# A state-space layer with a tree layer behind it on one core: constant products, the first delta, two broadcasts and the last leaf stages take other places

## What is computed

```python
h = layernorm(x) * (1 + ca) + sa
xp, z = split(h @ W_in)                       # 256 channels each
u = silu(causal_depthwise_conv(xp))           # 4 taps
dt_r, Bm, Cm = split(u @ W_xp, [8, 24])       # 8, 16 and 16 columns
delta = softplus(dt_r @ W_dt + dt_bias)
# for each channel e and each of 16 states n, over the 2048 positions t:
#   state = exp(-delta * exp(A_log)) * state + delta * Bm * u;   y = sum_n state * Cm
x = x + ga * ((y + u * D_skip) * silu(z)) @ W_out
h = layernorm(x) * (1 + cb) + sb
gate = sigmoid(h @ Wq.T @ routers.T)          # 255 nodes of a binary tree of depth 8
leaf_prob = product of gate or 1 - gate along the path to each of 256 leaves
x = x + gb * (leaf_prob @ leaf_values @ Wout_w.T + Wout_b)
```

## Time and profile before

| | |
|---|---|
| median of 3 runs (lowest, highest) | 488.26 us (485.96, 488.31) |
| the profiled execution, its span | 488.33 us, 486.5 us |
| VectorE busy | 447.5 us, 92% of the span |
| GpSimd busy | 422.0 us, 87% |
| TensorE busy with products | 404.0 us, 83% |
| ScalarE busy | 377.1 us, 77% |
| mean granted TensorE clock | 0.961 of full speed |

### The profile page before, as it was taken

How to read it: one execution, slowest core, us unless ns; L and a number is a source line. 1 busy time by engine, 2 the same in 40 slices (tenths; PEclk the granted TensorE clock), 3 DMA queues, 4 the chain that set the end, 5 groups by cost and what they waited for, 6 DMA issues and landing times. The chain is left out here.

```text
span 486.5 us, 6739 instructions
## 1 busy us (share of the span) xinstructions
PE 404.0 (83%) x2164; PEld 274.6 (56%) x2164; DVE 447.5 (92%) x539; ACT 377.1 (77%) x690; POOL 422.0 (87%) x236
## 2 busy tenths in 40 slices
PE   6979765997679887997889888997789887688596
PEld 3546544584547545584647546574647555566374
DVE  6687999999999999999999899989999899999872
ACT  4376985499777998698967999699966997777825
POOL 6148899999999989999899889999899889999910
PEclk9979997899799999999989999999999998799999
DMA  6684019200632019300633018300632027300001
GB/s 168 159 279 182 1 30 343 88 0 1 232 140 88 1 22 350 113 0 2 217 154 109 2 34 340 108 2 0 247 143 93 1 54 319 108 2 22 0 1 43
DMA packets 24146, 51.06 MB, mean 105 GB/s; under 512 B 4521, under 2 KB 14256, under 8 KB 20016
## 3 DMA queue, kind: packets, MB, share of 16 engines
q1 hardware_dynamic: 24112, 50.64, 30.4%
HBM read 48.01 MB, written 2.62 MB: 104 GB/s over the span
## 5 line engine op out<-in xcount | busy, mean ns | idle before, releaser
L606 POOL TENSOR_TENSOR hc<-h,c_rows 128x1024 f32<-128x1024 f32 x127 | 297.9, 2364 | 23.8 <-DVE h L1382 22.7
L1382 DVE TENSOR_TENSOR_SCAN h<-dA,state,dbu 128x512 f32<-128x512 f32 x192 | 234.0, 1270 | 7.3 <-ACT dA L697 7.3
L697 ACT ACTIVATE dA<-delta,a_neg 128x512 f32<-128x512 f32 x256 | 172.7, 684 | 38.1 <-DVE h L1382 37.7
L1123 PEld LDWEIGHTS yb<-ident,hc 128*128 128x128 f32 x1024 | 127.8, 146 | 65.5 <-issue 40.8
L1123 PE MATMUL yb<-ident,hc 128*128 128x128 f32 x1024 | 151.4, 282 | 12.6 <-POOL hc L606 12.6
L1395 DVE TENSOR_TENSOR dbu<-du,bb 128x1024 f32<-128x1024 f32 x88 | 105.9, 1203 | 6.6 <-PE bb L1148 5.8
L593 POOL TENSOR_TENSOR dbu<-du,b_rows 128x1024 f32<-128x1024 f32 x40 | 94.6, 2365 | 4.4 <-DMA b_rows<-bc_dram 4.4
L1382 DVE TENSOR_TENSOR_SCAN h<-dA,dbu 128x512 f32<-128x512 f32 x64 | 74.2, 1209 | 2.7 <-ACT dA L697 2.6
L1148 PE MATMUL bb<-b_parts,sel 128*128 128x512 bf16 x88 | 35.0, 398 | 34.5 <-DVE dbu L1395 33.2
L1023 PE MATMUL mf<-f_hT,w_conv 128*128 128x512 f32 x112 | 55.0, 616 | 1.8 <-ACT zu L757 1.2
L1148 PEld LDWEIGHTS bb<-b_parts,sel 128*128 128x128 bf16 x88 | 8.8, 100 | 47.3 <-DVE dbu L1395 27.8
(11 more groups left out here) (207 smaller groups left out, 520.5 us busy)
## 6 DMA issues: line engine op xcount, KB each, us to landing
...
```

What stands on the lines that cost most here:

```text
L606: nc.gpsimd.tensor_tensor(hc[:, pair % RC, :, :], h[:, pair % RH, :, :], c_rows[:, q, n % NQ, :].unsqueeze(1).broadcast_to([P, HALVES, T]) ...
L697: nc.scalar.activation(dA[ke % RD][:, :], delta[:, ge % 2, half, :], ACT.Exp, scale=a_neg[:, half, n:n + 1]).then_inc(s_dA, 1)
L1123: last = nc.tensor.matmul(bank[:, tile], hc[:, pair % RC, half, tile], ident[:, :], start=False, stop=n == N - 1, is_transpose=True, skip_ ...
L1382: v.tensor_tensor_scan(h[:, pair % RH, half, :], dA[k % RD][:, :], dbu[:, pair % RW, half, :], start, ALU.mult, ALU.add).then_inc(s_scan, 1)
```

## The change

It has four parts. (1) The preparation of group 0: eleven instead of seven start products, and further ones of the same kind ("fillers") behind the modulation products, the turn of x, ahead of the first fill and, in group 7's tail, where the leaf product's second half was. The second group of modulation products, the gate products and the folding move from between and behind the u products to behind the xd product, the folding to behind the first fill; the folded matrix is copied by ScalarE ahead of its third exponential. The first two deltas come from the eight dt rows of xd and W_dt as it is (`w_dt8`; rows 32 to 39), for which two DMAs are added. ScalarE copies xd before VectorE casts it, and VectorE casts from that copy. (2) The gate values are worked out at step 19 of group 0 (`S_GATES`). (3) The fills of pairs 3 and 4 are issued at k = 1 and 4 instead of 3 and 5 (`SOONER`). (4) In group 7 the leaf stages of group 5 go to the f side, at steps 4 to 9 instead of 12 to 16; group 6's tail comes two steps sooner, and its leaf product is all issued within the loop. Waits and reads that name the side (`leaf_side`, `due`) follow.

The diff, with repeated renamings of the side left out:

```diff
@@ -68,7 +68,7 @@
...
-    B_HI, C_ROW, B_MID, B_LO = 0, N, 64, 96
+    B_HI, C_ROW, DT_ROW, B_MID, B_LO = 0, N, 32, 64, 96
@@ -103,20 +103,23 @@
...
-    WARM_START = 7
+    WARM_START = 11
+    S_GATES = 19
+    SOONER = {1: 3, 4: 4}
...
     BY_HAND = 1
-    LAST_T = (("yt", 0, -1, (6,)), ("yt", 1, -1, (8,)), ("out", 0, -1, (10,)), ("lp", 0, -2, (12,)),
-              ("lp", 1, -2, (14,)), ("ff", 0, -2, (16,)), ("tr", 0, -1, (19,)), ("node", 0, -1, (21,)),
-              ("node", 1, -1, (23,)), ("lp", 0, -1, (27,)), ("lp", 1, -1, (29,)), ("ff", 0, -1, (STEPS,)))
-    LAST_SP = {2: -2, 25: -1}
+    LAST_T = (("yt", 0, -1, (6,)), ("yt", 1, -1, (8,)), ("out", 0, -1, (10,)), ("tr", 0, -1, (17,)),
+              ("node", 0, -1, (19,)), ("node", 1, -1, (21,)), ("lp", 0, -1, (25,)), ("lp", 1, -1, (27,)),
+              ("ff", 0, -1, (29, 30)))
+    LAST_F = (("lp", 0, -2, (4,)), ("lp", 1, -2, (6,)), ("ff", 0, -2, (8, 9)))
+    LAST_SP = {2: -2, 23: -1}
     TOKENS = (slice(0, T // 2), slice(T // 2, T))
-    LAST_STATS, LAST_RSTD, LAST_OFF, LAST_XHAT = 14, 16, 16, 17
+    LAST_STATS, LAST_RSTD, LAST_OFF, LAST_XHAT = 13, 14, 14, 15
...
-        if side == "t" and g == LAST:
-            return LAST_T
+        if g == LAST:
+            return LAST_T if side == "t" else LAST_F
@@ -158,6 +166,7 @@
...
         w_dt = sb("w_dt", [R, DI])
+        w_dt8 = sb("w_dt8", [DT_ROW + R, DI])
@@ -390,7 +399,7 @@
...
-        n_late, n_dt, n_col, n_xp, n_rest = 2, 2, 4, 4, 14
+        n_late, n_dt, n_col, n_xp, n_rest = 2, 2, 4, 6, 14
@@ -424,8 +433,9 @@
...
             sp.wait_ge(s_wz, 1)
-            for row, first, width in ((B_HI, R, N), (C_ROW, R + N, N), (B_MID, R, N), (B_LO, R, N)):
+            for row, first, width in ((DT_ROW, 0, R), (B_HI, R, N), (C_ROW, R + N, N), (B_MID, R, N), (B_LO, R, N)):
                 load(w_xp[:, :, row:row + width], xp_v[:, :, first:first + width], s_wxp)
+            load(w_dt8[DT_ROW:DT_ROW + R, :], W_dt, s_wxp)
@@ -668,7 +678,7 @@
...
                 nc.scalar.preload_act_table_set("softplus")
-                act.wait_ge(s_hi, 1)
+                act.wait_ge(s_xd0, 1)
@@ -693,6 +703,12 @@
...
                             act.wait_ge(s_aneg, 1)
+                            act.wait_ge(s_gatec, 1)
+                        if ke == 2:
+                            act.wait_ge(s_wdtp, 1)
+                            nc.scalar.activation(w_xdt[:, :, :],
+                                                 dA[2][:, 0:HALVES * DI].rearrange("p (h e) -> p h e", h=HALVES),
+                                                 ACT.Copy).then_inc(s_wdt, 1)
@@ -852,10 +870,6 @@
...
                 nc.scalar.preload_act_table_set("softplus")
-                wait_job(act, "t", "ff", 0, t - 1)
-                nc.scalar.activation(xs[:, (t - 1) * TILES:t * TILES, :],
-                                     job("t", "ff", 0, t - 1)[1][:, :].rearrange("p (i d) -> p i d", d=DM),
-                                     ACT.Copy).then_inc(s_read["t"], 1)
@@ -910,7 +924,7 @@
...
                 for hh in range(HALVES):
-                    last = nc.tensor.matmul(dA[0][:, hh * DI:(hh + 1) * DI], w_dtin_t[:, hh * P:(hh + 1) * P],
+                    last = nc.tensor.matmul(dA[2][:, hh * DI:(hh + 1) * DI], w_dtin_t[:, hh * P:(hh + 1) * P],
@@ -927,25 +941,21 @@
...
             def dt_product(half):
-                for hh in range(HALVES):
-                    last = nc.tensor.matmul(yb[half][:, :], w_xdt[:, hh, half * P:(half + 1) * P],
-                                            zu[:, 0, HALVES + hh, :], start=hh == 0, stop=hh == HALVES - 1)
-                last.then_inc(s_dt0, 1)
+                nc.tensor.matmul(yb[half][:, :], w_dt8[DT_ROW:DT_ROW + R, half * P:(half + 1) * P],
+                                 xd[DT_ROW:DT_ROW + R, :], start=True, stop=True).then_inc(s_dt0, 1)
...
                 modulation_products(yb[0], 0)
+                keep_warm_on(dA[0], 1)
...
                 turn_x(mb["f"][0], s_tr0)
-                dt_weight_transposes()
+                keep_warm_on(dA[0], 2)
...
                 u_product(0)
-                pe.wait_ge(s_wlate, 16 * n_late)
-                modulation_products(mb["t"][0], 3)
-                dt_weight_products()
+                dt_weight_transposes()
                 u_product(1)
-                gate_products()
@@ -953,13 +963,16 @@
...
                 last.then_inc(s_xd0, 1)
-                pe.wait_ge(s_wdt, 1)
-                dt_product(0)
+                pe.wait_ge(s_wlate, 16 * n_late)
+                modulation_products(mb["t"][0], 3)
+                gate_products()
...
                 pe.wait_ge(s_xdc, 1)
+                pe.wait_ge(s_modc, 1)
+                dt_product(0)
+                pe.wait_ge(s_hi, 1)
...
                                  skip_group_check=True).then_inc(s_r1, 1)
-                pe.wait_ge(s_gatec, 1)
@@ -1043,6 +1056,8 @@
...
                         pe.wait_ge(s_silu, g + 1)
+                        if (side, g) == ("f", 1):
+                            pe.wait_ge(s_wdt, 1)
@@ -1133,8 +1148,14 @@
...
                     kf, ks = k + AHEAD_FILL, k - LAG_SUM
-                    if 0 <= kf < K and kf % HALVES == 0 and kf // HALVES % N not in POOL_N:
-                        pair = kf // HALVES
+                    pair = kf // HALVES if 0 <= kf < K and kf % HALVES == 0 else None
+                    if k in SOONER:
+                        pair = SOONER[k]
+                    elif pair in SOONER.values():
+                        pair = None
+                    if pair is not None and pair % N not in POOL_N:
+                        if pair == 0:
+                            keep_warm(1)
@@ -1147,6 +1168,8 @@
...
                                          start=True, stop=True).then_inc(s_fill, 1)
+                        if pair == 0:
+                            dt_weight_products()
@@ -1181,8 +1204,8 @@
...
                 y_sum(K - 5)
+                wait_read(pe, "f", "ff", 0, t - 2)
                 hold_rows(0)
-                product(t - 1, "t", "ff", 0, 0, 2)
@@ -1206,7 +1229,7 @@
...
                     last.then_inc(s_out7, 1)
-                product(t - 1, "t", "ff", 0, 1, 2)
+                keep_warm_on(dA[1], 3)
@@ -1280,7 +1303,7 @@
...
                 dve.wait_ge(s_gatep, 1)
-                copy = v.tensor_copy(gate_raw[:, :, :, :], yb[1][:, :].rearrange("p (b i d) -> p b i d", b=BATCH, i=2))
+                copy = v.tensor_copy(gate_raw[:, :, :, :], dA[0][:, :].rearrange("p (b i d) -> p b i d", b=BATCH, i=2))
@@ -1314,17 +1337,13 @@
...
                                         ALU.mult).then_inc(s_wconv, 1)
-                dve.wait_ge(s_wdtt, 1)
-                v.tensor_copy(w_dtin_t[:, :], bb[0][0:R, 0:DI]).then_inc(s_wdtc, 1)
...
                 v.tensor_scalar(a_neg[:, :, :], a_neg[:, :, :], -1.0, None, ALU.mult).then_inc(s_aneg, 1)
-                mod_columns(mb["t"][0], 3)
-                dve.wait_ge(s_wdtp, 1)
-                v.tensor_copy(w_xdt[:, :, :],
-                              dA[0][:, 0:HALVES * DI].rearrange("p (h e) -> p h e", h=HALVES)).then_inc(s_wdt, 1)
+                dve.wait_ge(s_wdtt, 1)
+                v.tensor_copy(w_dtin_t[:, :], bb[0][0:R, 0:DI]).then_inc(s_wdtc, 1)
@@ -1332,13 +1351,12 @@
...
                 stats(3, f_bn, f_mv[:, 3, :, :], s_fvar)
+                dve.wait_ge(s_xdc, 1)
+                v.tensor_copy(b_parts[:, 0, :], xd[:, :]).then_inc(s_hi, 1)
+                mod_columns(mb["t"][0], 3)
                 gates()
-                dve.wait_ge(s_xd0, 1)
-                v.tensor_copy(b_parts[:, 0, :], mb["f"][0][:, :]).then_inc(s_hi, 1)
-                gate_signs()
...
                 v.tensor_copy(b_parts[B_MID:P, 0, :], mb["f"][0][B_MID:P, :]).then_inc(s_mid, 1)
-                gate_values()
@@ -1395,6 +1413,9 @@
...
                                         ALU.mult).then_inc(s_dbu, 1)
+                    if g == 0 and s == S_GATES:
+                        gate_signs()
+                        gate_values()
```

33 lines of the change are left out of this document (19 added, 14 removed).

## The result

The changed kernel takes 492.43 us in the median of six executions (488.82 to 494.11); the kernel before took 487.42 beside it (485.96 to 488.40). The ratio is 1.0103, with a 95% interval of 1.0075 to 1.0130: slower by 1%, where 484.4 us and 0.8% faster had been forecast. The profiled execution took 492.69 us, with a mean granted clock of TensorE of 0.944 (0.961 before).

A forecast was written before the change was run, and what follows sets the result against it. VectorE was taken as the bound, nearly every scan and product standing behind the last. From 488.3 us, -4.6 - 2.9 + 4.6 - 1.0 = -3.9 gave 484.4 us, range 480.2 to 488.0.

The forecast's parts named there:

- A: Up to the first scan: gaps filled, u products at full clock, shorter deltas; first scan sooner, -4.6 us.
- (b): Rival, before the first u product: the start products and fillers don't lift TensorE's clock; 486.2 us, chance 0.17.
- (d): Rival, preparation: TensorE keeps its lower clock until the second u product is through; 490.7 us, chance 0.05.
- B: Group 0, steps 0 to 10: three of VectorE's waits for broadcasts go; -2.9 us, bounds -1.5 and -3.5.
- C: Step 19 of group 0: four gate instructions between two scans, plus one GpSimd multiplication waited for; +4.6 us.
- D: Group 7 and end: softplus -1.1, first gating -1.3, moved leaf stages +1.4; -1.0 us, bounds -2.8 and +1.7.

The follow-up runs named there:

- fillers: The changed kernel with three constant products instead of one ahead of the first fill, three behind the first z product, five behind the second; 489.40 us, 1.0050.
- before_warm: The kernel before with eleven constant products around the first fill and z products, nothing of the change; 486.60 us, 0.9985.
- leaf_behind_alone: The kernel before with the change's group 7 alone, group 5's leaf stages at steps 11 to 16, behind the turns; 485.15 us, 0.9957.
- gates_alone: The kernel before with only the gate values moved to step 19 of group 0; 488.72 us, 1.0027.
- scale_first: The changed kernel with GpSimd reading the gate values at step 19, ahead of its multiplication for pair 9; 493.97 us, a single run.
- leaf_alone: The kernel before with only the change's tables of group 7 and its end; 490.97 us, 1.0051.
- warm_only_front: The changed kernel with eleven constant products around the first fill and z products, gate values among the casts, group 7 as before; 484.53 us, 0.9941.
- warm_leaf_gates: The changed kernel with eleven added constant products, group 5's leaf stages behind the turns, gate values among the casts; 482.06 us (0.9890), again 483.97 us (0.9915).

## Why the prediction was wrong

The ratios of all versions to the kernel before, side by side:

| | gates at step 19 | gates among the casts |
|---|---|---|
| new prologue, leaf stages ahead of the turns | 1.0103 | 1.0072 |
| and fillers | 1.0050 | not run |
| leaf stages behind the turns | 1.0031 | 0.9986 |
| and fillers | 0.9955 | 0.9890, 0.9915 |

- **A, -4.6: right.** -4.96, with both u products at 3.7 us and less, the copy of xd at 17.95 and the first exponential at 23.61. Rivals (b) and (d) did not happen in their form.
- **B, -2.9: this step failed.** It came out at +4.45 (from -4.96 to -0.51). Two of the four waits for broadcasts went, as said (1.11 and 1.45 us), the 0.35 stayed, but waits of 1.95, 0.55 and 1.01 us for exponentials stand in the same stretch now. The sentence that failed is that "the first wait (for pair 1) follows both z products and stays as it is or shrinks by some 0.6, if TensorE is not slowed there". TensorE was slowed, for twice as long as before and on the very pieces that now stood in the chain. The comparison of -0.51 with the -5.78 of fillers puts that at 5.3 us in the profiles. With the clock held B is still only -0.8: VectorE arrives five us sooner, the fold stands ahead of the z products, and the wait for pair 1 is 2.46 instead of 1.13. I had taken these at zero.

  And that compares with a kernel before whose own clock fell. Where it did not (before_warm, leaf_behind_alone, gates_alone), the old order runs from the first scan to scan 12 faster by 2.2 to 2.5 us, so at full clock in both the new order loses some 1.5 us there. The gain that B counted was in part the clock's: without a fall the wait of 1.11 us is absent in the old order as well, and only the one of 1.45 (1.21 at full clock) is the order's. The bound of -1.5 for "TensorE again at 0.50" left no room for 13.6 us of half clock on the pieces that VectorE waits for; the measured value lay 6 us outside it. Rival (d) comes nearest: it had the low clock with the u products, one stage too early, took B at -1.5 for it, and had a chance of 0.05.
- **C, +4.6: right at its place**, +4.67, by the instruction that was named, behind one multiplication of GpSimd (scale_first). But as a term of the sum it was too large: in gates_alone 1.7 us came back, 0.6 at step 31 and 1.1 in group 1, since waits of the kernel before stood behind it, and in the changed kernel 1.1. By the medians the move costs 1.3 us in the kernel before (1.0027), 1.5 in the changed kernel and 2 to 3 in the repaired one. I had written that in the groups between nothing moves.
- **D, -1.0: wrong sign**, +1.3. The leaf stages cost 2.9 us at steps 10 to 13 (4.6 in leaf_alone), where I had taken 1.4 with 3.0 as the bound: TensorE's half clock at 419 to 426 us, which the kernel before has there too, fell on the first of them, and the copies of two turns waited, not of one. The softplus came out as said (1.1). At the end the first gating gained 0.45 us instead of 1.3: the leaf product only moved ahead in the same chain of TensorE.
- **The sum by what was measured:** -4.96 + 4.45 + 4.67 - 1.09 + 1.31 = +4.38 us, the difference of the two profiles' spans (the times, 492.69 and 488.33, differ by 4.36; the medians by 5.0). Here -1.09 is what came back between step 20 and group 7 in this kernel.

What stays open: why the clock falls at 22 us in one execution of the same instructions and not in another. Whether a gap ahead of it, the phase at which the program starts or something outside the core decides was not tried. The traces give two hints. In all eleven profiles with such a fall the stretch at full clock ahead of it was equally long, wherever it began. No run took the eleven start products back to seven, so it isn't shown that the sooner rise brought the sooner fall. And the moment of the rise differs from execution to execution. With the fillers the clock fell early in the two profiles where it had risen at 4.8 and 4.9 us, and not in the three where it rose at 5.8, 6.4 and 6.6. Here are the start products of warm_only_front (fell), of which the last ones ran fast already, and of warm_leaf_gates (did not):

```profile
1.31 4.31 PE L896 MATMUL bb<-idle 128*128 128x512 bf16 x11 [1.31 <-POOL idle L507]
```

```profile
1.31 4.88 PE L893 MATMUL bb<-idle 128*128 128x512 bf16 x11 [1.31 <-POOL idle L508]
```

In the prologue of before it fell where it had risen at 13.2 and 13.5 us (before, leaf_alone) and not at 13.9 (leaf_behind_alone). That points to the phase, with few profiles, and proves nothing.
